# Self-attention: one projection piece between the scores and the turning of the probabilities

## What is computed

```python
x = x + _L0_attn_ref(_layernorm(x, axis=-1), ...)
# in _L0_attn_ref, H = 16 heads of HD = 64:
h = x * jax.lax.rsqrt(jnp.mean(x * x, axis=-1, keepdims=True) + EPS) * norm_w
q, k, v = (proj(w_q), proj(w_k), proj(w_v))
ll = jnp.einsum('bhnqd,bhnkd->bhnqk', qw, kw) * scale
ll = jnp.where(cm, ll, NEG).reshape(B, H, S, W)
...
attn = jax.nn.softmax(jnp.concatenate([ll, lg], axis=-1), axis=-1)
o = jnp.einsum('bhnqk,bhnkd->bhnqd', a_loc, vw).reshape(B, H, S, HD)
...
return x + jnp.einsum('bse,ed->bsd', o, w_out)
```

## Time and profile before

| | |
|---|---|
| median of 3 runs | 2175.17 us (2170.39 to 2175.69) |
| the profiled execution | 2167.51 us |
| its span, first to last instruction | 2165.8 us |
| mean granted TensorE clock over the span | 0.928 |
| self-attention, about | 0 to 1410 us |
| one loop period, about | 169 us |
| busy share of the span | PE 90%, DVE 59%, ACT 45%, POOL 44% |
| mean granted clock, 386.9 to 1232.3 us | 0.98 |

### The profile page before, as it was taken

One profiled execution on the slowest core, in us unless ns is written; L12 is line 12 of the kernel. 1 busy time (PEld: TensorE's weight loads), 2 busy tenths in 40 slices (PEclk: granted clock), 3 DMA queues, 4 the chain that ended last, 5 costly groups with the idle time before them and its releaser, 6 DMA issues. The chain is left out here.

```text
span 2165.8 us, 34295 instructions
## 1 busy us (share of the span) xinstructions
PE 1954.0 (90%) x10249; PEld 1450.7 (67%) x10249; DVE 1286.0 (59%) x3621; ACT 983.9 (45%) x2471; POOL 951.5 (44%) x1900
## 2 busy tenths in 40 slices
PE   4699999999999999999999999768999999788898
PEld 3577677667667667757757767438888888655443
DVE  5476476467567557557647646327888888735401
ACT  2455355445446436536535636327565655223210
POOL 2354454454454455455454435427555656220000
PEclk9799999999999999999999999879887878579999
DMA  5612111111211211121121121030123212140000
GB/s 201 245 59 88 61 67 60 70 69 59 89 69 59 80 66 72 60 79 59 71 88 59 50 72 65 10 95 28 36 78 123 70 53 64 69 181 1 0 1 19
DMA packets 60098, 154.08 MB, mean 71 GB/s; under 512 B 11347, under 2 KB 12371, under 8 KB 51336
## 3 DMA queue, kind: packets, MB, share of 16 engines
q1 hardware_dynamic: 59272, 149.78, 19.8%
q0 software_dynamic: 640, 2.10, 0.3%
HBM read 125.64 MB, written 26.21 MB: 70 GB/s over the span
## 5 line engine op out<-in xcount | busy, mean ns | idle before, releaser
L479 POOL TENSOR_TENSOR units<-units,fixed 128x1 f32<-128x1 f32 (+1 forms) x384 | 232.8, 606 | 644.4 <-ACT probs L544 644.3
L544 ACT ACTIVATE probs<-probs,units 128x512 f32<-128x512 f32 (+3 forms) x512 | 284.9, 557 | 492.2 <-DVE units L654 492.2
L662 DVE TENSOR_TENSOR pt_lo<-pt_bank,pt_hi 128x512 fp32r<-128x512 f32 (+2 forms) x384 | 223.0, 599 | 182.6 <-ACT pt_hi L554 181.8
L484 POOL TENSOR_SCALAR probs<-probs,units 128x512 f32<-128x512 f32 (+3 forms) x512 | 276.7, 547 | 0.0
L786 PE MATMUL pt_bank<-ident,probs 128*128 128x128 f32 x1280 | 189.5, 286 | 61.3 <-POOL probs L484 57.3
L654 DVE CUSTOM_DVE_ANT_0 probs<-s_bank,bias 128x512 f32<-128x512 f32 (+3 forms) x512 | 227.1, 487 | 13.3 <-issue 13.1
L761 PE MATMUL pj_bank<-ht_hi,wqk 128*128 128x512 f32 x512 | 221.0, 432 | 9.7 <-DMA wqk<-wqk_split 8.0
L843 PE MATMUL pj_bank<-w_o,o_t 128*128 128x512 f32 x512 | 225.7, 592 | 1.4 <-DVE o_t L667 1.4
L762 PE MATMUL pj_bank<-ht_hi,wqk 128*128 128x512 f32 x512 | 207.5, 405 | 0.0
L763 PE MATMUL pj_bank<-ht_lo,wqk 128*128 128x512 f32 x512 | 207.3, 405 | 0.0
L786 PEld LDWEIGHTS pt_bank<-ident,probs 128*128 128x128 f32 x1280 | 139.6, 143 | 97.5 <-issue 61.5
(11 more groups left out here) (258 smaller groups left out, 3916.8 us busy)
## 6 DMA issues: line engine op xcount, KB each, us to landing
wqk<-wqk_split SPq DMA_DIRECT2D x63, 1024.0 KB, 4.9
xt<-x SPq DMA_DIRECT2D x36, 256.0 KB, 2.9
xb<-in_x SPq DMA_DIRECT2D x8, 1024.0 KB, 7.1
wqk_split<-w_stage SPq DMA_DIRECT2D x16, 512.0 KB, 6.0
xr<-in_x SPq DMA_DIRECT2D x32, 256.0 KB, 4.4
x<-xr SPq DMA_DIRECT2D x32, 256.0 KB, 2.1
am<-in_L_ffn_attention_mask SPq DMA_DIRECT2D x8, 1024.0 KB, 5.2
out<-x SPq DMA_DIRECT2D x32, 256.0 KB, 2.1
```

Source lines behind the costliest of these rows:

```text
L479: nc.gpsimd.tensor_tensor(rden[:, slot, 0:k], den[:, slot, 0:k], minus[:, 0:k], ALU.pow).then_inc(rden_ready, 1)
L484: ins = nc.gpsimd.tensor_scalar(probs[:, slot, c0:c0 + nk], probs[:, slot, c0:c0 + nk], rden[:, slot, k:k + 1], 1.0, ALU.mult, ALU.mult)
L544: ins = nc.scalar.activation(probs[:, slot, c0:c0 + nk], probs[:, slot, c0:c0 + nk], ACT.Exp, bias=nmax[:, slot, k:k + 1], scale=-1.0, acc ...
L662: nc.vector.tensor_tensor(dst, src, hi.bitcast(F32), ALU.subtract).then_inc(pt_taken, 1)
```

## The change

In the slots without values products (slot number not 1 modulo 3), the slot's first piece moves on TensorE from behind the turning to between the scores and the turning. The order of all pieces among themselves stays, and so does the order on the other engines. Slot 16 has no piece and slots 1, 4, ..., 22 stay as they are. A piece that does not exist in a written-out period is left out after the order was made: in period 0 that holds for the output pieces, so slot 5 has none, and in slot 6 nothing is moved, since its first piece is o3b; in period 7 it holds for the pieces of the next batch, so slots 20, 21 and 23 have none.

```diff
-        pe_order = engine_order(("s", "pv", "t"), PIECE_KINDS, ("ht", "score", "tw"))
+        pe_order = pe_slots()
...
+def pe_slots():
+
+    order = engine_order(("s", "pv", "t"), PIECE_KINDS, ("ht", "score", "tw"))
+    out = []
+    for slot in range(NG):
+        items = [a for a in order if a[3] == slot]
+        pieces = [a for a in items if a[0] in PIECE_KINDS]
+        if slot % 3 != 1 and pieces:
+            items.remove(pieces[0])
+            items.insert(1, pieces[0])
+        out += items
+    return out
```

## The result

The change makes the kernel slower. The median goes from 2172.65 us (2166.16 to 2184.99, 15 runs) to 2182.72 us (2172.72 to 2189.53, 15 runs), a ratio of 1.0042 with a 95% interval of 1.0028 to 1.0057. The forecast was 2164 us. The profiled execution takes 2178.01 us with a span of 2176.3 us, where the one before has 2167.51 and 2165.8.

A forecast was written before the change was run, and what follows sets the result against it. TensorE, busy 90% of the span, was taken as the bound, so only its waits could be won. 4.2 + 2.0 + 3.5 + 1.0 + 0.3 = 11.0 us from the 2175.2 us median gave 2164 us, range 2152 to 2174.

The forecast's parts named there:

- 1.4 - 0.7 = 0.7 us a period: Slot 8, six loop periods: q4a fills 1.4 us of wait, slot 6 passes on 0.7 us delay; 4.2 us won.
- so I book nothing for the clock: Slot 8, loop periods: idle stretch becomes 3.1 us, nearest row has granted clock 0.89, so no clock gain or loss.
- The bound beside it: Slot 8's clock: at most 1.8 us a period won, or 1.6 us lost in three periods going from 0.89 to 0.79.
- 0.5 us a period: Slots 15 to 18: 0.3 us from slot 15 plus 0.4 less 0.2 us; 3.5 us won in seven periods.
- brings the first turned bank some 0.2 us late: Slot 18: k7b ahead of the turning hides 0.66 us of wait but delays the following chain by 0.2 us.
- The rest: free: Slots 2, 3, 5, 9, 11, 12, 14, 20, 21, 23 (and 6): moving a piece without a wait costs nothing.
- The cover that I named: Slots without a wait: ScalarE's first cast comes some 2.6 us in; turning up to 0.3 us late, about 2 us spare.
- Slot 0: Wins 0.5 us in periods 1 and 7, 1.0 us together; in periods 2 to 6 the wait moves to slot 1.
- That VectorE waits for the turning: Slot 0, in the returned-waits rival: five periods lose 0.75 us each; sum 5.8 us, 2169 us; chance 0.28.
- The sign that I gave: Slot 1, periods 2 to 6: a wait for pt_lo of about 1.1 us instead of 0.6.
- 2.5 us booked in slots 8 and 15 to 18: Period 0: 2.0 us won in slot 8 (1.4 plus 0.6 for the clock), 0.5 us in slots 15 to 18.
- slower: Rival: slot 6 passes all 3.04 us of delay to slot 8's normalisation; 13 us lost, 2188 us; chance 0.08.

The follow-up runs named there:

- e1: Changed kernel with the piece moved only in slots 8 and 18; one run, 2170.57 us beside a median of 2170.91 us.
- e3: Changed kernel with the piece moved only in slots 2, 3, 5, 9, 11, 12, 14, 20 and 21; ratio 1.006, median 2183.12 us.
- e8: Kernel before, with one to three pieces moved ahead or between turnings in slots 9, 11, 12, 14, 20, 21, 23; one run, 2210.81 us beside 2170.63.
- e4: Changed kernel with the piece moved only in slots 0, 8, 15 and 17; ratio 0.9943, median 2158.0 us.
- e9: Changed kernel with slot 6 undone, o3b behind the turning again; ratio to before 0.9975, median 2171.08 us.
- e10: Changed kernel with the piece moved only in slots 8, 15 and 17; ratio 0.9929, median 2156.98 us.
- e6: Changed kernel plus VectorE's statistics put right behind the two maxima in slot 6; ratio 0.9852, median 2140.67 us.
- e2: Changed kernel with the piece moved only in slots 6 and 23; one run, 2188.93 us.
- e5: Kernel before, TensorE's order untouched, VectorE's statistics put right behind the two maxima in slot 6; ratio 0.9819, median 2133.58 us.

## Why the prediction was wrong, point by point

**Slot 8, "1.4 - 0.7 = 0.7 us a period": wrong, + 0.21 us.** The 1.4 us of q4a were right (e1). The delay through slot 6 was sized at 0.7 us and is 1.41. Two readings failed in what reaches ScalarE's copy. o3b's price of 3.04 us was the distance to the start of the next operation, but that row's first matmul then took 0.63 us to the next (611.27 to 611.90) where 0.32 is usual, so 0.3 us of o3b stood in the neighbour; the turning starts 3.54 us after o3b and not 3.04. And from the cast to the copy ScalarE needs 1.59 us, not 1.4. Together they put the copy 0.7 us later than forecast. That the wait on the normalisation came out at 3.15 us, as forecast (3.1), is luck: the normalisation was late by 1.41 us and not by 0.7, but slot 7 had grown by 0.46 us and took that much of it, and q4a filled 1.6 us and not 1.4.

The second part of the loss I had listed and set to nothing: the clock. Take the time from the turning's start to the end of the slot, less what the same rows need at full clock: 1.65 us for the two turnings with the time between their starts, and behind them 4.27 us for 18 matmuls or 2.85 us for 12. That leaves 2.0 us before (mean of six, 12.63 - 4.74 - 5.92), 1.9 in e1 (11.10 - 4.74 - 4.50) and 2.7 in the changed kernel (12.84 - 5.65 - 4.50). Sum: - 1.4 (q4a) + 0.9 (the turning at + 5.65 instead of + 4.74) + 0.7 (clock) = + 0.2 us. The step that failed is "so I book nothing for the clock". The bound beside it named what came: the three periods with a granted clock of 0.89 went to 0.79 in the 16 us window. By the same working their cost goes from 1.4 or 1.5 us to 2.5 or 2.6, and that of the other three from 2.4 or 2.5 to 2.8. Each mean is from one profile: it is 2.0, 2.1 and 2.4 us in the three kernels that leave slot 8's start and order alone (before, e3, e8), and 1.3 to 1.9 us in the four that move q4a with slot 6 as before (e1, e4, e9, e10).

The granted clock is 0.51 in the window from the turning on, the level of 1.2 GHz, after a wait of 3.15 us. The rule of the Trainium skill that the prediction cites (TensorE: Matmul & The Clock Gate, section "HAM oscillation — how this bites in real kernels"), half of the half-rate stretch, would make 3.5 us of this 7 us window, as an estimate. The trace gives 2.5 us in this period (12.69 - 5.65 - 4.50); part of the slowness falls into the second wait, which shrinks from 0.81 to 0.45 us. The measurement decides.

**Slot 7: not in the prediction, + 0.46 us.** The statistics stand ahead of the step on VectorE that frees o3's bank (line 696), so when they come 1.4 us late, k3a waits for the bank; with the statistics early the slot is back at 7.08 us (e6). I followed slot 6's delay to POOL, but not to what else is queued behind it on VectorE.

**Slots 15 to 18, "0.5 us a period" won: wrong, + 0.31 us.** The 0.5 us are real with slots 15 and 17 alone (- 0.69 + 0.18 in e10). The step that failed is k7b in slot 18: "brings the first turned bank some 0.2 us late". It comes 0.77 us late, the chain through cast and low part passes on 0.42 (e1), and in periods 2, 4 and 6 a lower clock (0.89 over the two slots) makes slots 18 and 19 another 1.2 us longer. What brings it isn't shown: e1 has the same waits of 1.18 and 0.86 us there, at full clock in all periods. I had called the chain fixed, and then let only 0.2 us of delay into it.

**"The rest: free": wrong, + 0.66 us a period** for the nine slots without a wait and slot 6. The cover that I named does hold, since no later wait appeared. But TensorE itself is what bounds these slots, and there a different order of the same work costs 0.04 to 0.11 us a slot. Ten slots, six periods: 4 us. Slot 23, also on that list, is 0.5 us longer, and slot 0 behind it gives that back.

**Slot 0: right.** Periods 1 and 7 win 0.49 and 0.45 us, and in periods 2 to 6 slot 1 takes back what slot 0 wins (e4, e10). That VectorE waits for the turning, as the row's releaser had it, is refuted: in period 5 of the changed kernel VectorE starts 2.17 us into the slot, and the turning only at + 2.40. The sign that I gave, a wait of about 1.1 us in slot 1, shows with slot 0's piece moved alone at the turn (1.03 to 1.38 us in e4); in the changed kernel it is 0.48 to 0.81 us, since slot 0's scores start late there. VectorE has been idle for 2.5 to 3.1 us at each taken turn, in every kernel; what makes it so no run here shows.

**Period 0: 2.5 us booked in slots 8 and 15 to 18, and period 1 starts 0.15 us late.** Slot 8 wins 3.46 us where I booked 2.0, but not by the sum that I made. With q4a moved and the clock still low it wins 1.0 to 1.3 us (e1, e4, e10), less than my 1.4. In the changed kernel and in e9 the turning also starts 0.5 us earlier in the slot, the wait is down to 1.2 us, and the slot runs at full clock. Slot 4 loses 3.29 us, at a granted clock of 0.50:

```profile
94.00:98.00 4.00, 4.00 (x14) 3.61 (x14) 1.18 (x7) 1.31 (x4) 2.91 (x7) 0.50 1.08 267
```

It takes 8.0 to 8.5 us in three kernels (after, e6, e9) and 4.7 to 5.8 in the others. The three move the pieces of slots 0, 2 and 3; e4 moves that of slot 0 without the others and e3 those of slots 2 and 3 without slot 0, and neither shows it. What brings the low clock there stays open.

**The rivals.** The "slower" one named the right place, slot 6, and its time, 2188 us, is nearer to the result than the forecast. Its mechanism was too strong: not 3.04 but 1.41 us get through. I gave it 0.08 because it had to carry the whole loss by itself. The loss came from one delay sized at half, and from several terms set to nothing, which all pointed the same way.

## What to carry to other kernels

Filling a wait moves what stands behind the filler, and where the waited-for chain begins two slots earlier, the same edit there can delay it. Follow a moved step down every queue to the slot that waits, and then ask for the first thing on that chain that can go earlier: moving the statistics removed the wait that the change only filled, and won 39 us, where filling it in slots 8, 15 and 17 won 15. Where the busiest engine had no wait, no reordering of its row was free here: 0.03 to 0.12 us a slot, and over 1 us where the late turning made a later slot wait (e8). Move only what stands in front of a wait.

## What the runs showed of the hardware

- One and the same slot with the same start of the turning (+ 4.71 us) took 11.60, 11.99, 12.85 and 13.48 us in different periods of e3. So the low clock behind one and the same gap differs from time to time; what decides isn't shown. Behind waits of about 2.3 us it fell into the next slot in two periods of e4 and one of e10, and in period 4 of e9 it didn't come at all (slots 8 and 9 at 9.31 and 6.32 us). Mean costs over six periods: 2.0 to 2.4 us after waits of 3.8 and up to 0.8 us (before, e3, e8), 1.3 to 1.9 us after about 2.3 us (e1, e4, e9, e10), 2.7 us after 3.15 us (after), 2.3 us after 4.74 us (e2), and none where only 0.16 us of wait is left (e5). A longer gap doesn't simply cost more.
- The rest of the program behind the end of slot 22 of period 7, unchanged in all kernels, differs by up to 15 us between profiles: 788.5 us before (2165.8 - 1377.35) and 803.8 us in e4 (2168.4 - 1364.63). One profile's span can't judge a change of 10 us here; the lengths of the slots can.
- The first 128x512 matmul of a projection piece, behind scores or a turning, takes 0.31 to 0.34 us to the next start, its followers 0.23. The first transpose behind a piece takes 0.12 us and its followers 0.11. A moved piece adds one start of 0.34 us in place of 0.23, and the turning's first start gets shorter, 0.12 us in place of 0.17 (slot 11: + 0.05 us).
- TensorE's first matmul behind a taken turn of the loop is 0.2 to 0.7 us late when a piece stands ahead of the last turning, and now and then 0.1 to 0.4 us late without; the two theories that were tried for it failed.
